# Second-layer scatters of a two-layer graph network: from one group at a time to bursts of two groups, one burst behind the sums

## The reference

```python
h = x @ W1 + b1                                   # layer 0
e = concatenate([h[dst], h[src] - h[dst]], axis=-1)
m = relu(relu(e @ W2 + b2) @ W3 + b3)
x = layernorm(x + relu(segment_max(m, dst)))
msgs = edge_weight[:, None] * x[dst]              # layer 1
AX = segment_sum(msgs, src)
x = layernorm(x + AX @ W.T + b)
```

## Time and profile before

| what | value |
|---|---|
| median of 3 runs | 2623.38 us |
| the profiled execution's own time | 2633.35 us |
| its span, first to last instruction | 2631.6 us |
| layer 1's first half, from PE's first to last matmul | 1536.1 to about 2248.8 us |
| in it, DVE / ACT / POOL / PE busy in 1700 to 2100 us | 176 / 200 / 225 / 331 of 400 us |
| mean granted TensorE clock of the span | 0.917 |

### The profile page before, as it was taken

One profiled execution on the slowest core, in us unless ns is written; L12 is line 12 of the kernel. 1 busy time (PEld: TensorE's weight loads), 2 busy tenths in 40 slices (PEclk: granted clock), 3 DMA queues, 4 the chain that ended last, 5 costly groups with the idle time before them and its releaser, 6 DMA issues.

```text
span 2631.6 us, 62039 instructions
## 1 busy us (share of the span) xinstructions
PE 1940.8 (74%) x15568; PEld 1701.2 (65%) x15568; DVE 1619.5 (62%) x4450; ACT 817.0 (31%) x2385; POOL 1279.1 (49%) x1300
## 2 busy tenths in 40 slices
PE   4616677777777777777785378888888888788884
PEld 4615565565565555565564378877888778788884
DVE  3416666666666666666679544444444444688887
ACT  0312233233332332332332234445554555100003
POOL 6444566666666666666643435555555555100000
PEclk7757999999999999999997589999999999899997
DMA  4215555555555555555553156766666677788885
GB/s 114 81 46 153 142 148 147 151 148 148 150 147 150 146 150 151 146 148 150 148 147 91 32 179 209 216 207 208 216 214 210 214 214 217 225 268 267 262 266 175
DMA packets 534341, 447.34 MB, mean 170 GB/s; under 512 B 64731, under 2 KB 499383, under 8 KB 534240
## 3 DMA queue, kind: packets, MB, share of 16 engines
q1 hardware_dynamic: 342788, 208.10, 29.1%
q0 software_dynamic: 53312, 138.17, 16.5%
q10 hardware_dynamic: 138140, 100.06, 12.7%
HBM read 300.43 MB, written 145.64 MB: 170 GB/s over the span
## 4 chain that ended last, share of the span: by engine, by line
PE 43%; issue 19%; SPq 11%; another core or an unknown queue 9%; DVE 8%; ACT 3%; DMA 2%; DVEq 2%; POOL 2%; ACTq 1%; POOLq 0%
SPq L494 8%; PE z_ps L1385 5%; PE t_ps L1394 4%; PE m_ps L1372 4%; PE z_ps L1460 4%; PE t_ps L1460 4%; PE m_ps L1484 4%; PE m_ps L1373 4%; PE z_ps L1484 3%; PE t_ps L1484 2%; DVE run L989 2%; POOL whole L430 2%; SPq L490 1%; SPq L483 1%
## 5 line engine op out<-in xcount | busy, mean ns | idle before, releaser
L423 POOL DMA_INDIRECT whole<-q_tab,src_ti x784 | 760.9, 971 | 503.2 <-remote 243.0
L440 POOL DMA_INDIRECT tab<-whole,row_at x392 | 410.1, 1046 | 355.9 <-ACT whole L698 175.3
L1119 DVE TENSOR_SCALAR whole<-row_bc,node_id 128x768 f32<-128x768 uint8 x392 | 233.5, 638 | 390.1 <-PE t_ps L1460 110.4
L1460 PE MATMUL z_ps<-win,whole 128*128 128x128 f32 x2352 | 302.9, 286 | 71.6 <-DVE whole L1119 21.8
L1372 PE MATMUL m_ps<-ident,whole 128*128 128x128 f32 x1568 | 324.3, 290 | 29.1 <-issue 17.1
L635 ACT ACTIVATE m<-m_ps,bias 128x512 f32<-128x512 f32 x196 | 134.7, 687 | 644.2 <-remote 591.9
L1460 PEld LDWEIGHTS z_ps<-win,whole 128*128 128x128 f32 x2352 | 282.7, 198 | 78.0 <-issue 41.6
L1460 PE MATMUL t_ps<-win,whole 128*128 128x128 f32 x2352 | 294.7, 280 | 50.6 <-issue 25.8
L1373 PE MATMUL m_ps<-oh,win 128*128 128x128 f32 x1568 | 316.2, 285 | 0.6 <-issue 0.6
L1460 PEld LDWEIGHTS t_ps<-win,whole 128*128 128x128 f32 x2352 | 274.4, 193 | 54.1 <-issue 30.3
L1372 PEld LDWEIGHTS m_ps<-ident,whole 128*128 128x128 f32 x1568 | 259.1, 207 | 62.6 <-issue 62.5
(11 more groups left out here) (277 smaller groups left out, 3128.3 us busy)
## 6 DMA issues: line engine op xcount, KB each, us to landing
win<-p_tab SPq DMA_DIRECT2D x784, 64.0 KB
seg_tab<-run_e ACTq DMA_DIRECT2D x196, 256.0 KB
win<-xw_tab SPq DMA_DIRECT2D x784, 64.0 KB
whole<-tab SPq DMA_DIRECT2D x220, 200.0 KB
whole<-tab ACTq DMA_DIRECT2D x220, 200.0 KB
row_bc<-seg_row_tab SPq DMA_DIRECT2D x196, 128.0 KB
row_bc<-rel_tab SPq DMA_DIRECT2D x196, 96.0 KB
whole<-q_tab,src_ti POOLq DMA_INDIRECT x784
```

What stands on the lines that cost most here:

```text
L423: pool.indirect_dma_start(qg[:, g % RING, j, :], None, q_tab[:, :], IOA(ap=src_ti[:, t:t + 1], axis=0)).then_inc(q_ld[g % RING], 16)
L440: pool.indirect_dma_start(tab[:, :], IOA(ap=row_at[0:FR, k:k + 1], axis=0), fat[0:FR, k % RR, :], None).then_inc(fat_st[k % RR], 16)
L1119: last = V.tensor_scalar(pick[:, s, j, :], row_bc[:, r, 0:GK * SLOTS], node_id[:, j:j + 1], None, ALU.is_equal)
L1460: last = mm(fat_bank[s][0:FR, c, q * P:(q + 1) * P], lhsT=pick[:, s, j, (c * SL + q) * FR:(c * SL + q + 1) * FR], rhs=win[:, r % UN, CK * ...
```

## The change

- **POOL** works in bursts of two groups (four scatters). Before burst u (groups 2u and 2u+1) it waits until PE has summed the whole of burst u+1, that is all groups up to 2u+3.
- **PE and ACT** have three bank pairs for the sums (`m1_ps` is added), so group g waits for ACT's copy of group g - 3.
- **DVE** has four buffers of `pick` and `later`; `picks` of group g waits for the matmuls of group g - 4. The order later, picks, keys within a group and the waits of `keys` are as before. It waits once for all of `xw_ps` before its first group, since `pick` now lies where one of PE's operands was.
- **SP** loads a chunk's 256 rows with one DMA of 128 KB from the base of its first tile (two per group, not four). A second tile's indices are moved by the difference of the two bases (`opened`) and not by 128. SP goes two groups at a time: it waits for the sums of groups up to 2u+1, loads chunks for 2u+4 and 2u+5, waits for the picks up to 2u+3, and loads the index rows for 2u+6 and 2u+7.

```diff
-        pick = l1(HX * D, 2 * CK * GK * SLOTS).rearrange("p (s j e) -> p s j e", s=2, j=CK)
+        pick = l1(0, UN * CK * GK * SLOTS).rearrange("p (s j e) -> p s j e", s=UN, j=CK)
...
-        later = junk[0:WIDE, :, :].rearrange("p t d -> p (t d)").bitcast(BF)[:, 0:2 * GK * FR].rearrange("p (s c j) -> p s c j", s=2, c=GK)
+        later = junk[0:WIDE, :, :].rearrange("p t d -> p (t d)").bitcast(BF)[:, 0:UN * GK * FR].rearrange("p (s c j) -> p s c j", s=UN, c=GK)
...
-        fat_bank = [z_ps, t_ps]
+        fat_bank = [z_ps, t_ps, m1_ps]
...
-        PAIRS0 = [16 * (ROWS0[r] + (IT if r < UN else 0)) for r in range(RB)] + [16 * GT * (WINS0[r] + IT) for r in range(UN)]
+        PAIRS0 = [16 * (ROWS0[r] + (IT if r < UN else 0)) for r in range(RB)] + [16 * (GT * WINS0[r] + GK * IT) for r in range(UN)]
...
-            for k in range(K):
-                if k % GK == 0:
-                    pool.wait_ge(at_ev, k // GK + 1)
-                    pool.wait_ge(keys_done, k // GK + 1)
-                pool.wait_ge(fat_ev, k + 1)
-                pool.indirect_dma_start(tab[:, :], IOA(ap=row_at[0:FR, k:k + 1], axis=0), fat[0:FR, k % RR, :], None).then_inc(fat_st[k % RR], 16)
+            for u in range(G // 2):
+                if u + 1 < G // 2:
+                    pool.wait_ge(fat_ps, 2 * GK * (u + 2))
+                pool.wait_ge(at_ev, 2 * u + 2)
+                pool.wait_ge(keys_done, 2 * u + 2)
+                for k in range(2 * GK * u, 2 * GK * (u + 1)):
+                    pool.wait_ge(fat_ev, k + 1)
+                    pool.indirect_dma_start(tab[:, :], IOA(ap=row_at[0:FR, k:k + 1], axis=0), fat[0:FR, k % RR, :], None).then_inc(fat_st[k % RR], 16)
...
+            def chunks(g):
+                if g % 4 == 0:
+                    _, bases[1] = nc.values_load_multi_w_load_instructions(
+                        base_row[0:1, GT * g:GT * (g + 4)].rearrange("a (k j) -> a k j", j=CK)[:, :, 0], engines=bass.OrderedEngineSet([mybir.EngineType.SP]),
+                        min_val=0, max_val=NP, skip_runtime_bounds_check_because="a count of segments opened before a tile is below the count of nodes")
+                for c in range(GK):
+                    sp.dma_start(win[:, g % UN, CK * c:CK * (c + 1), :], xw_tab[ds(bases[1][GK * (g % 4) + c], CK * P), :].rearrange("(j p) d -> p j d", p=P)
+                                 ).then_inc(win_ld[g % UN], 16)
+
             sp.wait_ge(xw_st, 16 * (HX // GT))
             for g in range(UN):
-                windows(xw_tab, g)
-            for g in range(UN, G):
-                sp.wait_ge(fat_ps, GK * (g - UN + 1))
-                sp.sem_inc(sp_waited, 1)
-                rows1(g)
-                windows(xw_tab, g)
+                chunks(g)
+            for u in range(-1, G // 2):
+                if u >= 0 and u + 2 < G // 2:
+                    sp.wait_ge(fat_ps, 2 * GK * (u + 1))
+                    sp.sem_inc(sp_waited, 1)
+                    for g in (2 * u + UN, 2 * u + UN + 1):
+                        chunks(g)
+                if u + 3 < G // 2:
+                    sp.wait_ge(pick_done, 2 * (u + 1) + 2)
+                    for g in (2 * u + UN + 2, 2 * u + UN + 3):
+                        rows1(g)
...
             def fat_copy(i, r):
                 for c in range(GK):
-                    act.wait_ge(fat_ps, GK * grp(i, r) + c + 1)
-                    if old(i, r - UN):
-                        act.wait_ge(fat_st[GK * (r % UN) + c], 16 * i_of(i, r))
+                    k = (GK * r + c) % RR
+                    act.wait_ge(fat_ps, GK * grp(i, r, RING) + c + 1)
+                    if old(i, r - UN, RING):
+                        act.wait_ge(fat_st[k], 16 * i_of(i, r, RING))
                     for q in range(SL):
-                        last = nc.scalar.activation(fat[0:FR, GK * (r % UN) + c, q * KW:q * KW + D], fat_bank[r % 2][0:FR, c, q * P:(q + 1) * P], ACT.Copy,
-                                                    scale=slot_cols[:, ds(2 * SL * (GK * grp(i, r) + c) + 2 * q + 1, 1)])
+                        last = nc.scalar.activation(fat[0:FR, k, q * KW:q * KW + D], fat_bank[r % 3][0:FR, c, q * P:(q + 1) * P], ACT.Copy,
+                                                    scale=slot_cols[:, ds(2 * SL * (GK * grp(i, r, RING) + c) + 2 * q + 1, 1)])
                     last.then_inc(fat_ev, 1)
...
+            base_of = base_f[:, :].rearrange("p (k j) -> p k j", j=CK)
+            link(V.tensor_tensor(opened[:], base_of[:, :, 1], base_of[:, :, 0], ALU.subtract))
             odd = rel[:, :].rearrange("p (k j e) -> p k j e", j=CK, e=P)[:, :, 1, :]
-            V.tensor_scalar(odd, odd, float(P), None, ALU.add).then_inc(rel_ready, 1)
+            V.tensor_tensor(odd, odd, opened[:, :].unsqueeze(2).to_broadcast([PA, TA // CK, P]), ALU.add).then_inc(rel_ready, 1)
...
             def picks(i, r):
 
-                s = r % 2
                 dve.wait_ge(row_ld[r], 16 * (ROWS0[r] + i + 1))
-                if old(i, r - 2):
-                    dve.wait_ge(fat_ps, GK * (grp(i, r - 2) + 1))
+                if old(i, r - UN):
+                    dve.wait_ge(fat_ps, GK * (grp(i, r - UN) + 1))
                 for j in range(CK):
-                    last = V.tensor_scalar(pick[:, s, j, :], row_bc[:, r, 0:GK * SLOTS], node_id[:, j:j + 1], None, ALU.is_equal)
+                    last = V.tensor_scalar(pick[:, r, j, :], row_bc[:, r, 0:GK * SLOTS], node_id[:, j:j + 1], None, ALU.is_equal)
                 last.then_inc(pick_done, 1)
...
             def later_blocks(i, r):
-                s = r % 2
-                if old(i, r - 2):
-                    dve.wait_ge(at_ps, grp(i, r - 2) + 1)
-                V.tensor_tensor(later[:, s, :, :], iota_f[0:WIDE, 0:FR].unsqueeze(1).to_broadcast([WIDE, GK, FR]),
+                if old(i, r - UN):
+                    dve.wait_ge(at_ps, grp(i, r - UN) + 1)
+                V.tensor_tensor(later[:, r, :, :], iota_f[0:WIDE, 0:FR].unsqueeze(1).to_broadcast([WIDE, GK, FR]),
                                 firsts[:, ds(GK * grp(i, r), GK)].unsqueeze(2).to_broadcast([WIDE, GK, FR]), ALU.is_ge).then_inc(later_done, 1)
...
+            dve.wait_ge(xw_ps, HX // GT)
...
             def fat_rows(i, r):
-                s = r % 2
                 pe.wait_ge(pick_done, grp(i, r, RING) + 1)
-                pe.wait_ge(win_ld[r % UN], 16 * GT * (WINS0[r % UN] + i_of(i, r, RING) + 1))
+                pe.wait_ge(win_ld[r % UN], 16 * (GT * WINS0[r % UN] + GK * (i_of(i, r, RING) + 1)))
                 for c in range(GK):
-                    if old(i, r - 2, RING):
-                        pe.wait_ge(fat_ev, GK * grp(i, r - 2, RING) + c + 1)
+                    if old(i, r - 3, RING):
+                        pe.wait_ge(fat_ev, GK * grp(i, r - 3, RING) + c + 1)
                     for q in range(SL):
                         for j in range(CK):
-                            last = mm(fat_bank[s][0:FR, c, q * P:(q + 1) * P], lhsT=pick[:, s, j, (c * SL + q) * FR:(c * SL + q + 1) * FR],
+                            last = mm(fat_bank[r % 3][0:FR, c, q * P:(q + 1) * P], lhsT=pick[:, r % UN, j, (c * SL + q) * FR:(c * SL + q + 1) * FR],
                                       rhs=win[:, r % UN, CK * c + j, :], start=j == 0, stop=j == CK - 1)
                     last.then_inc(fat_ps, 1)
```

More of the change, by code:

```diff
@@ L157, in gnn_kernel @@
         base_i = sb("base_i", [PA, TA], I32)
+        opened = sb("opened", [PA, TA // CK])
         opens = rel
@@ L688, in row_at_ev @@
             def row_at_ev(i, r):
-                act.wait_ge(at_ps, grp(i, r) + 1)
-                nc.scalar.activation(row_at[0:FR, ds(GK * grp(i, r), GK)], s_ps[0:FR, r % 2, 0:GK], ACT.Identity, bias=iota_p[0:FR, :]).then_inc(at_ev, 1)
+                act.wait_ge(at_ps, grp(i, r, RING) + 1)
+                nc.scalar.activation(row_at[0:FR, ds(GK * grp(i, r, RING), GK)], s_ps[0:FR, r % 2, 0:GK], ACT.Identity, bias=iota_p[0:FR, :]).then_inc(at_ev, 1)
             def fat_copy(i, r):
                 for c in range(GK):
-                    act.wait_ge(fat_ps, GK * grp(i, r) + c + 1)
-                    if old(i, r - UN):
-                        act.wait_ge(fat_st[GK * (r % UN) + c], 16 * i_of(i, r))
+                    k = (GK * r + c) % RR
+                    act.wait_ge(fat_ps, GK * grp(i, r, RING) + c + 1)
+                    if old(i, r - UN, RING):
+                        act.wait_ge(fat_st[k], 16 * i_of(i, r, RING))
                     for q in range(SL):
-                        last = nc.scalar.activation(fat[0:FR, GK * (r % UN) + c, q * KW:q * KW + D], fat_bank[r % 2][0:FR, c, q * P:(q + 1) * P], ACT.Copy,
-                                                    scale=slot_cols[:, ds(2 * SL * (GK * grp(i, r) + c) + 2 * q + 1, 1)])
+                        last = nc.scalar.activation(fat[0:FR, k, q * KW:q * KW + D], fat_bank[r % 3][0:FR, c, q * P:(q + 1) * P], ACT.Copy,
```

(20 more changed lines are left out.)

## The result

The changed kernel takes 3083.78 us (median of 4 runs, 3082.2 to 3086.67), the kernel before 2623.93 us beside it: 1.174 times as long, 95% interval 1.171 to 1.178. Forecast were 3025 us, 401 more than before; measured are 460 more. The profiled execution spans 3081.6 us, 450.0 more than that of before.

The account below looks back on a forecast made before the run. PE was taken to be near its limit, with slack from index-row waits and SP's queue. 96 x (7.2 + 3.38 + 0.82 - 7.28) plus tail gave 401 us more, 3034, or 3025 from the median; range 2855 to 3200.

Parts of the forecast that it names:

- The ring: Layer 1's first half: scatters, landing, keys, picks and PE's group 2u+5 wait in a circle, 10.6 us per pair against 7.28.
- The fast rival (4): Keys of group 2u+4 don't hold picks of 2u+5: a pair runs at PE's 6.12 us, 2517 us; chance 0.06.
- React: From the end of PE's sums to the waiting engine's start, here POOL's burst: 1.20 us a round.
- L: From the second scatter's start to its landing: 3.38 us, midway between the quiet row's 2.59 and nearer loaded row's 4.17.
- PE's term: Length of PE's group 2u+5 within the round: 2.94 us plus the price of a lowered clock, 3.76 forecast.
- The clock: Idle PE slows its group 2u+5: 0.82 us a round, half the 1.65 that one 2.46 us gap cost.
- Rival 3: PE's group 2u+5 starts cold in each round and takes 5.46 us: 3187 us in all; chance 0.17.
- DVE's term: From the start of DVE's keys through later and picks to PE's start: 1.80 us a round.
- The tail: After PE's last group two bursts are still open: 10.16 us where it was 4.53, so +5.6 us.
- What was removed: Fewer window issues, earlier index rows, more buffers and banks: alone at most -111 us, a pair at 6.12 us.

## Why the prediction was right, and where its sizes were off

- **The ring.** Right. Keys behind the landing, picks behind the keys, PE's group 2u+5 behind the picks, the next burst behind that group: the profile shows each handover, and opening the ring at two different places (keys, POOL's wait) takes the slowdown away each time. POOL's loop alone brings it. The fast rival (4) was what the change would have given without the ring: a pair at 6.12 us, 2517 us. With the keys moved it comes to 6.5 us a pair and 2563.
- **React, 1.20 us.** Mis-sized: 0.33, as the burst follows 0.28 us behind most groups. It made the forecast 0.87 us a round too long. I had read it from one place, off DVE's picks and ACT's copy. Both also wait for something else there (index rows, a landing), so the end of PE's group need not have been what released them. The same trace had shorter ones: of ACT's 199 copies behind idle time, 35 start within 0.2 us of the last matmul of their chunk. The clock is not the reason either, since with PE kept busy the term is 0.33 too.
- **L, 3.38 us.** 3.58 on average (2.80 to 4.25). The reason for the middle between the quiet row and the nearer loaded one, the chunk loads leaving with the burst, is shown: with an eighth of their bytes L is 2.86 on chip 1, where the changed kernel has 3.62. I expected 65 to 90 us from that; it was 101, 96 x (0.76 + 0.29), since PE's term fell as well. That the shorter idle time in front (3.3 us for 4.1) made it fall is likely but not shown.
- **The clock, 0.82 us.** The term that was most mis-sized: PE's group took 4.97, not 3.76, so the clock cost 2.03 us a round and not 0.82. (From group to group PE stood idle for 4.1 us, forecast were 4.6.) Rival 3, cold in each round, gave 2.52 and was nearer than my value. The Trainium skill's rule in "TensorE: Matmul & The Clock Gate", section "HAM oscillation — how this bites in real kernels", is that a wait for data in each round can make each round start cold. The trace agrees in that none of the 95 groups on the ring took less than 4.28 us; only every second one took the 5.2 to 5.5 us of a group that is cold throughout. Nor does the idle time in front give the price by itself. In the run with small chunk loads, gaps of 2.9 to 3.9 us stood before groups of 4.2 to 4.6 us and gaps of 3.3 to 3.9 before groups of 5.5. The second trace of the kernel before has this group, at a granted clock of 0.50:

```profile
2233.48 5.49 PE L1460 MATMUL t_ps<-win,whole 128*128 128x128 f32 x24 [1.16 <-DVE whole L1119]
```

  In front of it PE was idle for 0.36, 0.96 and 1.16 us, with 0.7 us of matmuls between. So half of the 1.65 us that one row had cost was a size that no row supported.
- **Luck in the total.** The clock was 1.21 us a round too cheap (+116 us), L 0.20 too short (+19), the reaction 0.87 too long (-84) and DVE's term 0.04 (-4). With a right reaction and the same clock the forecast would have been some 84 us lower, about 2940. That 3025 lies 59 us from 3083.78 is owed in part to two errors that point opposite ways; what was foreseen is the ring.
- **The tail.** 4.7 us for 5.6, since its react term was too long too.
- **What was removed.** The waits for index rows did go, as said. What the loads, buffers and banks are worth shows only with the ring open and POOL per group: 0.6% on chip 14, 1.2% on chip 4. On chip 14 the one load per chunk alone gives 0.5% of it.

## A version that beats both

The changed kernel with keys two groups later: 0.974 of the kernel before on chip 14, 0.995 on chip 4, where that is hardly a gain. With POOL per group instead it is 0.994 and 0.988. On chip 14 bursts are worth 2.1%: both kernels have the late keys, and with bursts it is 2562.59 us, without 2616.69. On chip 4 bursts with late keys took 0.7% longer than POOL per group without them (2198.17 against 2182.5); there the two were not varied one by one.

## What to carry to other kernels

When a wait is moved later, follow every queue behind it until a chain either ends or comes back to the wait. If it comes back, its length is a floor for the round, whatever each engine's busy share says, and one group's shift in any link can open it. Idle time that a ring makes in front of its own matmuls is paid twice, since the clock drops; so add up the ring's length with its matmuls at the low clock.

## What the runs showed of the hardware that I had not expected

- **Chips differ on the same program:** 2210.56 us on chip 4, 2629.45 and 2628.07 on chips 1 and 14, 19% more. The changed kernel with POOL per group has a trace on both kinds, spans of 2179.4 and 2609.6 us. Of the 430 us between them 308 lie before layer 1's first window matmul (1226.6 and 1534.7), 121 in the first half of layer 1, and 1 in the second half. In 400 to 1000 us POOL issued 465 gathers on chip 4 and 389 on chip 14. In layer 1's first half PE stopped for more than 0.1 us within a group 96 times on chip 14, 49 us in all, and never on chip 4. Instructions alone take the same: a scatter's median is 0.97 us on both, a group of PE 2.92 to 2.94. What stretches the time on chips 1 and 14 stays open. That bursts help only there does too.
- **Work that nobody needs can pay:** 14 matmuls per round, 3.3 us of PE, held the granted clock at 1.00 and made the group behind them 2.97 us long on average. Without them it took 4.97 in the changed kernel and 5.06 with bursts alone.
- **The same gap does not cost the same each time:** in the run with small chunk loads, 3.3 to 3.9 us from group to group stood before groups of 4.2 to 4.6 us and before groups of 5.5, where 2.94 is the length at full clock. In the changed kernel the two lengths come in turns.
- **A 200 KB scatter lands 2.6 to 5.3 us after its start**; in the rounds of the changed kernel it lets the keys go after 2.80 to 4.25 us.
